# Last cross attention: where the value products, the totals and the context copies stand in a turn

## The chip, the cores and the metric

The kernel runs on one core of one Trainium2 chip. The metric is the device time of one execution in microseconds (us), lower is better. Engines: TensorE (PE, with its weight loads as PEld), VectorE (DVE), ScalarE (ACT), GpSimd (POOL), and SyncE (SP), which issues DMAs. Each engine works through its own list of instructions in order and waits on semaphores for the others.

## The reference, cut to what matters

The whole computation is four layers of cross attention and feed-forward on `x` of 8 x 256 x 128, all in float32. The change lies in the fourth layer's cross attention. Its context is `ctx_2048`, 8 x 1601 x 256, and a learned null key and value are added, so there are 1602 keys.

```python
HEADS, DH = (16, 64)
q = _split_heads(jnp.einsum('bnd,df->bnf', x, Wq))
kv = jnp.einsum('bmc,cf->bmf', context, Wkv)
k, v = jnp.split(kv, 2, axis=-1)
k, v = (_split_heads(k), _split_heads(v))
...
k = jnp.concatenate((nk, k), axis=-2)
v = jnp.concatenate((nv, v), axis=-2)
q = q * scale
sim = jnp.einsum('bhid,bhjd->bhij', q, k)
attn = jax.nn.softmax(sim, axis=-1)
out = jnp.einsum('bhij,bhjd->bhid', attn, v)
...
out = jnp.einsum('bnf,fd->bnd', out, Wout)
```

A layer norm of the result follows, and it is added to `x`.

## The kernel before

The stages of the kernel run one after the other; `cross3` (L2215) is the sixth of seven, and all of the change is in its class `KeyMajorAttention` (L1761). It works in 64 turns: one for each of 8 batches and 8 pairs of heads (`PAIRS`). In a turn the scores of a pair are made with the keys on the 128 partitions: 13 blocks of 128 keys, two heads of 64 rows each, 256 queries as columns. Two blocks are a chunk (`CHUNKS` = 7).

The work on one pair is spread over three turns. In turn i:
- `pe_score` makes the scores of pair i, chunk by chunk (26 matmuls, L1930, each on 64 of the array's rows) into two halves of `psS`. ScalarE copies each chunk to `prob` (`act_keep`, L2035), and VectorE takes the running maximum over chunks (`dve_raise`, L2101), then the last one over the two halves (`dve_peak`, L2107). A half of `psS` is used again when both have read it: score chunk s waits for the copy and the raise of chunk s - 2.
- For pair i - 1 the softmax is made. `pe_turn_peak` (L1944) transposes the maxima into `psO` (called `peaks`), `dve_shift` (L2113) reduces them over the keys, `pe_spread_shift` (L1951) spreads the negative maxima over the partitions, again in `psO`. VectorE adds them to the scores (`dve_lower`, L2122, four parts for each head), ScalarE takes the exponential (`act_exp`, L2041, eight parts), and GpSimd adds the exponentials up over the blocks (`pool_sums`, L2187 to L2198).
- For pair i - 2 the values are met: `pe_meet` (26 matmuls, L1975, each on 64 of the array's columns) into `psT[:, 1, 0:S]`, and `pe_total` (L1960, two matmuls with ones, on 64 columns) sums the exponentials over the partitions into `psO`. `dve_invert` (L2128) takes the reciprocal, and `dve_divide` (L2136) multiplies. So the totals need `psO`, which the shift of the next pair holds until VectorE has lowered all eight parts, and the transposes of the maxima wait for the reciprocal.
- `pe_project` makes what the next turns need, in two banks (`psT[:, 0]` and `psM`) in turn: keys (L1897) and queries (L1900) of pair i + 1, values (L1907) of pair i - 1, in turns 4 to 6 of a batch the transposes of the next batch's context (L1889), and in turn 2 the output projection of the batch before (L1913). `due(i, at)` says what is made at which of eight places of a turn; its place in the list and its number settle the bank, and the bank who copies it out: bank 1 is ScalarE's (`act_take`, L2013 to L2024), bank 0 is VectorE's (`dve_take`, L2079 and L2081), but values always go to ScalarE.

A turn has four rounds (`for g in range(4)` in `pe_run`). Round g issues: values of `MEETS[g]` (chunks 0 and 1, 2 and 3, 4 and 5, 6), in the first round the transposes of the maxima, then the projections due at place 2g, in the first round the spreading of the shift, then two chunks of scores, then the projections due at 2g + 1. The totals stand at the head of the third round. ScalarE in a round: the copies due at 2g, the copies of two score chunks, the copies due at 2g + 1; and in the first and second round four exponentials each. VectorE's order is written out in `dve_run`.

The accumulating value products of a pair all lie in one bank region, so the values of the next pair wait for the divide (`out_done`).

Of the kernel before, what the change touches and what calls it, by code (L numbers as in the profile page):

```python
# [1760 lines left out]
class KeyMajorAttention:  # L1761
# [16 lines left out]
    MEETS = [range(0, 2), range(2, 4), range(4, 6), range(6, 7)]  # L1778
# [46 lines left out]
    def due(self, i, at):  # L1825
# [7 lines left out]
        if 0 <= b < B - 1 and p in (4, 5, 6) and at in (2, 3, 4) and (p - 4) * 3 + at - 2 < 8:  # L1833
            names.append(("ctx", b + 1, (p - 4) * 3 + at - 2))
        if at == 3 and p == 2 and b > 0:
            names = (names or [None]) + [("out", b - 1, 0)]
# [97 lines left out]
    def pe_turn_peak(self, pe, i):  # L1934
        nc = self.k.nc
        pe.wait_ge(*self.peaked(i + 1))
        if i >= 2:
            pe.wait_ge(*self.inverted(i - 1))
# [15 lines left out]
    def pe_total(self, pe, i):  # L1954
        nc = self.k.nc
        pe.wait_ge(*self.summed(14 * (i + 1)))
        if i + 1 < self.TURNS:
            pe.wait_ge(*self.lowered(8 * (i + 2)))
        for h in range(2):
            last = nc.tensor.matmul(self.peaks[h * self.HD:(h + 1) * self.HD, 0:S], self.ones[:], self.acc[i % 2][:, h, 0:S],  # L1960
                                    start=True, stop=True)
# [17 lines left out]
    def pe_run(self, pe):  # L1979
# [4 lines left out]
        for i in range(-1, T + 3):  # L1984
            scores, softmax, meets = 0 <= i < T, 0 <= i - 1 < T, 0 <= i - 2 < T
            for g in range(4):
                if meets and g == 2:
                    self.pe_total(pe, i - 2)
                if meets:
                    for s in self.MEETS[g]:  # L1990
                        self.pe_meet(pe, i - 2, s)
                if softmax and g == 0:
                    self.pe_turn_peak(pe, i - 1)
                for name in self.due(i, 2 * g):
                    self.pe_project(pe, name)
                if softmax and g == 0:
                    self.pe_spread_shift(pe, i - 1)
                if scores:
# [8 lines left out]
    def act_take(self, act, name):  # L2007
# [13 lines left out]
        if kind == "ctx":  # L2021
            c, g = n // 4, n % 4
            w = BANK if g < 3 else KTAIL
            last = nc.scalar.copy(self.ctxT[of % 2][:, c, g * BANK:g * BANK + w], bank[:, 0:w])  # L2024
        last.then_inc(self.taken[self.number[name][0]].sem, 1)
# [22 lines left out]
    def act_run(self, act):  # L2048
# [3 lines left out]
        for i in range(-1, T + 1):  # L2052
            scores, softmax = 0 <= i < T, 0 <= i - 1 < T
            for g in range(4):
# [5 lines left out]
                if softmax and g < 2:  # L2060
                    for part in range(4):
                        self.act_exp(act, i - 1, g, part)
# [61 lines left out]
    def dve_invert(self, dve, i):  # L2124
# [3 lines left out]
        self.k.nc.vector.reciprocal(self.rtotal[:], self.peaks[:, 0:S]).then_inc(self.inverted.sem, 1)  # L2128
# [9 lines left out]
    def dve_run(self, dve):  # L2138
# [4 lines left out]
        for i in range(0, T + 3):  # L2143
# [12 lines left out]
            self.dve_take_at(dve, i, 2)  # L2156
            if softmax:
                self.dve_lower(dve, i - 1, 1, 2)
                self.dve_lower(dve, i - 1, 1, 3)
            if scores:  # L2160
# [1434 lines left out]
```

## Time and profile before

| | us |
|---|---|
| median of 3 runs | 4140.33 |
| lowest and highest | 4135.44, 4140.78 |
| profiled execution, device time | 4139.14 |
| its span in the trace | 4137.1 |
| TensorE busy in the span | 3676.2 (89%) |
| VectorE, ScalarE, GpSimd busy | 2683.1, 2281.6, 1350.8 |
| last cross attention, first scores to last divide | 2081.7 to 3874.2 |

Line numbers (L1975) are those of the kernel before. PE stands for matmuls, PEld for weight loads. Matmuls are pipelined, so their records overlap, and a float32 matmul leaves two records and two weight loads (the 26 value matmuls of a turn are 52 records). Where TensorE is busy all the time, the distances between the starts of neighbouring groups tell how long each group holds the engine.

### The profile page before, as it was taken

The numbers are of one execution on the slowest core, as the hardware profiler recorded it, in microseconds if no ns is written. First come the engines' busy times: TensorE is split into PE (matmuls) and PEld (weight loads), VectorE is DVE, ScalarE is ACT, GpSimd is POOL, SyncE is SP. The second block draws the span as 40 slices with busy tenths as digits, with TensorE's granted clock in tenths as the row PEclk, the third lists the DMA queues.
The fourth block names the chain that finished last, engine by engine and source line by source line (L and its number), as shares of the span: only waits on it lengthen the run. The fifth ranks groups of instructions, "written<-read, shape, count | busy, mean of one in ns | idle before, by whom it ended". The sixth has DMA issues, their size and how long they took to land. (4 is left out here: it accounts for less than half of the span.)

```text
span 4137.1 us, 72514 instructions
## 1 busy us (share of the span) xinstructions
PE 3676.2 (89%) x28012; PEld 2206.1 (53%) x28017; DVE 2683.1 (65%) x4526; ACT 2281.6 (55%) x3856; POOL 1350.8 (33%) x1655
## 2 busy tenths in 40 slices
PE   3699999889699985997799999999999999999654
PEld 2233333478444434674456666666666666666441
DVE  4799999544577736554356666666656666666647
ACT  2599999633377752222156566666656566656330
POOL 3011111220011104220045565555555556556310
PEclk7699999999799987998899999999999999999877
DMA  4332231002165401000100000000000000000010
GB/s 140 128 62 50 50 63 42 20 18 46 48 94 82 58 2 31 2 2 10 49 16 17 1 17 1 1 17 1 17 1 17 1 17 1 1 1 1 7 37 20
DMA packets 117718, 122.91 MB, mean 30 GB/s; under 512 B 19008, under 2 KB 95648, under 8 KB 116992
## 3 DMA queue, kind: packets, MB, share of 16 engines
q1 hardware_dynamic: 104184, 111.20, 12.2%
q10 hardware_dynamic: 13200, 7.16, 0.6%
q8 instruction: 221, 3.62, 0.4%
q14 instruction: 113, 0.93, 0.1%
HBM read 102.51 MB, written 15.68 MB: 29 GB/s over the span
## 5 line engine op out<-in xcount | busy, mean ns | idle before, releaser
L2101 DVE TENSOR_TENSOR att_highest.1<-att_highest.1,psS 128x1024 f32<-128x1024 f32 (+1 forms) x320 | 356.6, 1114 | 369.2 <-ACT prob_0.1 L2035 181.8
L869 DVE TENSOR_REDUCE att_peak.1<-psS 128x1 f32<-128x512 f32 (+1 forms) x1024 | 579.2, 633 | 19.8 <-PE psS L744 13.4
L839 ACT ACTIVATE att_probT.1<-psT 128x512 f32<-128x512 f32 (+1 forms) x682 | 366.6, 568 | 29.2 <-PE psT L773 9.9
L2192 POOL TENSOR_TENSOR key_sums_0.1<-key_sums_0.1,prob_0.1 128x512 f32<-128x512 f32 x256 | 326.5, 1275 | 28.7 <-POOL key_sums_0.1 L2192 0.4
L2192 POOL TENSOR_TENSOR key_sums_1.1<-key_sums_1.1,prob_1.1 128x512 f32<-128x512 f32 x256 | 325.8, 1273 | 28.7 <-POOL key_sums_1.1 L2187 0.4
L869 DVE TENSOR_REDUCE att_peak.2<-psS 128x1 f32<-128x512 f32 (+1 forms) x512 | 261.6, 568 | 78.7 <-PE psS L744 75.8
L790 PE MATMUL psM<-att_probT.1,quad_values.1 128*9 128x256 f32 (+1 forms) x3840 | 291.9, 382 | 0.2 <-issue 0.2
L744 PE MATMUL psS<-key_stack.1,query_stack.1 64*128 64x512 bf16 (+1 forms) x1024 | 253.6, 379 | 25.2 <-PEq L379 16.2
L2122 DVE TENSOR_TENSOR prob_0.1<-prob_0.1,psO 128x1024 f32<-128x1024 f32 (+1 forms) x256 | 244.0, 1016 | 49.0 <-PE psO L1951 49.0
L2122 DVE TENSOR_TENSOR prob_1.1<-prob_1.1,psO 128x1024 f32<-128x1024 f32 (+1 forms) x256 | 243.9, 1016 | 49.0 <-PE psO L1951 49.0
L2187 POOL TENSOR_TENSOR key_sums_0.1<-prob_0.1 128x512 f32<-128x512 f32 x64 | 82.0, 1282 | 576.1 <-ACT prob_0.1 L2041 576.1
L2035 ACT COPY prob_0.1<-psS 128x1024 f32<-128x1024 f32 (+1 forms) x224 | 203.8, 954 | 72.6 <-PE psS L1930 72.1
L2035 ACT COPY prob_1.1<-psS 128x1024 f32<-128x1024 f32 (+1 forms) x224 | 203.7, 954 | 71.8 <-PE psS L1930 71.4
L773 PE MATMUL psT<-query_stack.1,key_stack.1 64*128 64x256 bf16 x1279 | 212.9, 275 | 9.6 <-ACT att_probT.1 L839 9.5
L1897 PE MATMUL psM<-ctxT_0.1,wkv.1 128*128 128x512 f32 (+1 forms) x512 | 215.5, 544 | 2.7 <-ACT keyT_0.1 L2018 1.4
L1930 PE MATMUL psS<-qT_1.1,keyT_1.1 64*128 64x256 f32 x1664 | 214.5, 392 | 2.0 <-DVE att_highest.1 L2101 2.0
L1930 PE MATMUL psS<-qT_0.1,keyT_0.1 64*128 64x256 f32 x1664 | 214.5, 392 | 1.0 <-ACT keyT_0.1 L2018 0.7
L1907 PE MATMUL psT<-wkv.1,ctxT_1.1 128*128 128x128 f32 (+1 forms) x1664 | 214.7, 280 | 0.1
L1907 PE MATMUL psT<-wkv.1,ctxT_0.1 128*128 128x128 f32 (+1 forms) x1664 | 214.4, 280 | 0.0
L1907 PEld LDWEIGHTS psT<-wkv.1,ctxT_1.1 128*128 128x128 f32 (+1 forms) x1664 | 192.1, 187 | 37.5 <-issue 36.9
L1907 PEld LDWEIGHTS psT<-wkv.1,ctxT_0.1 128*128 128x128 f32 (+1 forms) x1664 | 192.1, 187 | 37.2 <-issue 36.1
L1897 PE MATMUL psM<-ctxT_1.1,wkv.1 128*128 128x512 f32 (+1 forms) x512 | 211.5, 536 | 0.0
(688 smaller groups left out, 7511.4 us busy)
## 6 DMA issues: line engine op xcount, KB each, us to landing
key_stack.1<-key_parts SPq DMA_DIRECT2D x384, 58.0 KB
key_stack.2<-key_parts SPq DMA_DIRECT2D x96, 200.1 KB
ctx_rows.1<-in_ctx_dram SPq DMA_DIRECT2D x8, 1536.0 KB
key_parts<-split_parts.2 SPq DMA_DIRECT2D x8, 1200.8 KB, 7.5
ctx_keys_0.1<-in_ctx_dram ACTq DMA_DIRECT2D x4, 768.0 KB
ctx_keys_1.1<-in_ctx_dram ACTq DMA_DIRECT2D x4, 768.0 KB
query_stack.1<-query_parts SPq DMA_DIRECT2D x192, 16.0 KB
ctx_values_0.1<-in_ctx_dram SPq DMA_DIRECT2D x4, 768.0 KB
```

The source lines that it names most:

```text
L744: self.k.nc.tensor.matmul(self.score_bank[m % 3][:, 0:w], self.queries(rows, g, h, s * P, P), self.keys(rows, g, h, c0, w), start=True, st ...
L773: last = self.k.nc.tensor.matmul(self.key_bank[(m + h) % 3][0:w, n * S:(n + 1) * S], self.keys(rows, g, h, col, w), self.queries(rows, g, ...
L790: last = self.k.nc.tensor.matmul(self.partial[32 * j:32 * j + self.hd + 1, :], self.vquad[0:w, q % 2, blk, j, :], self.probT[0:w, g % self ...
L839: self.k.nc.scalar.activation(probs[:, blks[0]:blks[-1] + 1, :].rearrange("p b q -> p (b q)"), bank[0:w, 0:len(blks) * S], ACT.Exp).then_i ...
L869: self.k.nc.vector.tensor_reduce(self.peak[:, 2 * h + s, c:c + 1], self.score_bank[m % 3][:, 0:w], AX_X, ALU.max).then_inc(self.peak_done. ...
L1897: last = nc.tensor.matmul(bank[:, 0:w], self.wkv[:, t, p * P:(p + 1) * P], self.ctxT[b % 2][:, t, n * BANK:n * BANK + w], start=(t == 0), ...
L1907: last = nc.tensor.matmul(bank[0:w, kb % 4 * P:(kb % 4 + 1) * P], self.ctxT[b % 2][:, t, kb * P:kb * P + w], self.wkv[:, t, at:at + P], st ...
L1930: last = nc.tensor.matmul(k.psS[:, 2 * (g % 2) + h, blk % 2 * S:(blk % 2 + 1) * S], self.keyT[i % 2][own, blk * P:(blk + 1) * P], self.qT[ ...
L2035: nc.scalar.copy(self.prob[i % 2][:, :, at:at + w], k.psS[:, 2 * (g % 2):2 * (g % 2) + 2, 0:w]).then_inc(self.kept.sem, 1)
L2101: self.k.nc.vector.tensor_tensor(own, old, new, ALU.max).then_inc(self.raised.sem, 1)
L2122: self.k.nc.vector.tensor_tensor(own, own, by, ALU.add).then_inc(self.lowered.sem, 1)
L2192: nc.gpsimd.tensor_tensor(acc, acc, own[:, h, c * BANK:(c + 1) * BANK], ALU.add).then_inc(self.summed.sem, 1)
```

## The change

- The values of a turn, all seven chunks of pair i - 2, are issued in one run at the turn's head, ahead of the transposes of the maxima. `MEETS` goes.
- The totals of pair i - 2 move from the head of the third round to the second round, behind its value projection and ahead of its scores. They are written to the second half of the values' bank, `psT[:, 1, S:2S]`, rather than to `psO`. Their wait for the lowering of the next pair goes, and so does the wait of the transposes of the maxima for the reciprocal.
- ScalarE makes two exponentials in each of the four rounds, not four in each of the first two.
- VectorE takes raises 2 and 3 ahead of the last two lowerings, then the reciprocal and the divide together, ahead of raises 4 and 5.
- The context transposes are due at places 0, 2 and 4 rather than 2, 3 and 4, the output projection at place 2 rather than 3. All of them come out in bank 1, and ScalarE copies them; VectorE takes none in the turns.

```diff
--- before.py
+++ after.py
@@ -1775,7 +1775,6 @@
     CHUNKS = (KB + 1) // 2
     NULL = KTAIL + 1
     KEYS = KB * P
-    MEETS = [range(0, 2), range(2, 4), range(4, 6), range(6, 7)]
 
     def __init__(self, k, mem):
         self.k = k
@@ -1830,9 +1829,9 @@
             names.append(("value", i - 1, at // 2))
         if at % 2 == 1 and i + 1 < self.TURNS:
             names.append(("key", i + 1, (3, 0, 1, 2)[at // 2]))
-        if 0 <= b < B - 1 and p in (4, 5, 6) and at in (2, 3, 4) and (p - 4) * 3 + at - 2 < 8:
-            names.append(("ctx", b + 1, (p - 4) * 3 + at - 2))
-        if at == 3 and p == 2 and b > 0:
+        if 0 <= b < B - 1 and p in (4, 5, 6) and at in (0, 2, 4) and (p - 4) * 3 + at // 2 < 8:
+            names.append(("ctx", b + 1, (p - 4) * 3 + at // 2))
+        if at == 2 and p == 2 and b > 0:
             names = (names or [None]) + [("out", b - 1, 0)]
         return names
 
@@ -1934,8 +1933,6 @@
     def pe_turn_peak(self, pe, i):
         nc = self.k.nc
         pe.wait_ge(*self.peaked(i + 1))
-        if i >= 2:
-            pe.wait_ge(*self.inverted(i - 1))
         if i >= 1:
             pe.wait_ge(*self.lowered(8 * i))
         for h in range(2):
@@ -1952,12 +1949,10 @@
         last.then_inc(self.spread.sem, 1)
 
     def pe_total(self, pe, i):
-        nc = self.k.nc
+        k, nc = self.k, self.k.nc
         pe.wait_ge(*self.summed(14 * (i + 1)))
-        if i + 1 < self.TURNS:
-            pe.wait_ge(*self.lowered(8 * (i + 2)))
         for h in range(2):
-            last = nc.tensor.matmul(self.peaks[h * self.HD:(h + 1) * self.HD, 0:S], self.ones[:], self.acc[i % 2][:, h, 0:S],
+            last = nc.tensor.matmul(k.psT[h * self.HD:(h + 1) * self.HD, 1, S:2 * S], self.ones[:], self.acc[i % 2][:, h, 0:S],
                                     start=True, stop=True)
         last.then_inc(self.totalled.sem, 1)
 
@@ -1983,18 +1978,19 @@
             self.pe_project(pe, ("ctx", 0, n))
         for i in range(-1, T + 3):
             scores, softmax, meets = 0 <= i < T, 0 <= i - 1 < T, 0 <= i - 2 < T
+            if meets:
+                for s in range(self.CHUNKS):
+                    self.pe_meet(pe, i - 2, s)
+            if softmax:
+                self.pe_turn_peak(pe, i - 1)
             for g in range(4):
-                if meets and g == 2:
-                    self.pe_total(pe, i - 2)
-                if meets:
-                    for s in self.MEETS[g]:
-                        self.pe_meet(pe, i - 2, s)
-                if softmax and g == 0:
-                    self.pe_turn_peak(pe, i - 1)
                 for name in self.due(i, 2 * g):
-                    self.pe_project(pe, name)
+                    if name is not None:
+                        self.pe_project(pe, name)
                 if softmax and g == 0:
                     self.pe_spread_shift(pe, i - 1)
+                if meets and g == 1:
+                    self.pe_total(pe, i - 2)
                 if scores:
                     for s in self.of_run(g):
                         self.pe_score(pe, i, s)
@@ -2022,6 +2018,8 @@
             c, g = n // 4, n % 4
             w = BANK if g < 3 else KTAIL
             last = nc.scalar.copy(self.ctxT[of % 2][:, c, g * BANK:g * BANK + w], bank[:, 0:w])
+        if kind == "out":
+            last = nc.scalar.copy(k.XN[:, of * QT:(of + 1) * QT, :].rearrange("p t d -> p (t d)"), bank[:, 0:S])
         last.then_inc(self.taken[self.number[name][0]].sem, 1)
 
     def act_keep(self, act, i, s):
@@ -2049,7 +2047,7 @@
         T = self.TURNS
         for n in range(1, 8, 2):
             self.act_take(act, ("ctx", 0, n))
-        for i in range(-1, T + 1):
+        for i in range(-1, T + 3):
             scores, softmax = 0 <= i < T, 0 <= i - 1 < T
             for g in range(4):
                 self.act_take_at(act, i, 2 * g)
@@ -2057,9 +2055,9 @@
                     for s in self.of_run(g):
                         self.act_keep(act, i, s)
                 self.act_take_at(act, i, 2 * g + 1)
-                if softmax and g < 2:
-                    for part in range(4):
-                        self.act_exp(act, i - 1, g, part)
+                if softmax:
+                    for part in (2 * g, 2 * g + 1):
+                        self.act_exp(act, i - 1, part // 4, part % 4)
 
 
 
@@ -2125,7 +2123,7 @@
         dve.wait_ge(*self.totalled(i + 1))
         if i >= 1:
             dve.wait_ge(*self.out_done(i))
-        self.k.nc.vector.reciprocal(self.rtotal[:], self.peaks[:, 0:S]).then_inc(self.inverted.sem, 1)
+        self.k.nc.vector.reciprocal(self.rtotal[:], self.k.psT[:, 1, S:2 * S]).then_inc(self.inverted.sem, 1)
 
     def dve_divide(self, dve, i):
         b, p = divmod(i, self.PAIRS)
@@ -2154,22 +2152,22 @@
                 self.dve_lower(dve, i - 1, 1, 0)
                 self.dve_lower(dve, i - 1, 1, 1)
             self.dve_take_at(dve, i, 2)
+            if scores:
+                self.dve_raise(dve, i, 2)
+            self.dve_take_at(dve, i, 3)
+            if scores:
+                self.dve_raise(dve, i, 3)
             if softmax:
                 self.dve_lower(dve, i - 1, 1, 2)
                 self.dve_lower(dve, i - 1, 1, 3)
-            if scores:
-                self.dve_raise(dve, i, 2)
-                self.dve_raise(dve, i, 3)
-            self.dve_take_at(dve, i, 3)
-            self.dve_take_at(dve, i, 4)
             if meets:
                 self.dve_invert(dve, i - 2)
+                self.dve_divide(dve, i - 2)
+            self.dve_take_at(dve, i, 4)
             if scores:
                 self.dve_raise(dve, i, 4)
                 self.dve_raise(dve, i, 5)
             self.dve_take_at(dve, i, 6)
-            if meets:
-                self.dve_divide(dve, i - 2)
             if scores:
                 self.dve_raise(dve, i, 6)
                 self.dve_peak(dve, i)
```

## Rows read from the trace of the kernel before

**Rows 1.** Busy time by stretches: stretch, length, busy us (records) by engine, PEclk, DMA share, GB/s.

```profile
2900.00:3100.00 200.00, 200.00 (x1375) 132.77 (x1374) 126.04 (x131) 121.15 (x173) 109.30 (x98) 1.00 0.03 9
```

**Rows 2.** Timeline of TensorE, an ordinary turn: start, busy us, engine, line, operation, out<-in, records.

```profile
3796.41 1.95 PE L1975 MATMUL psT<-prob_0.1,values_0.1 128*64 128x256 f32 x16
3798.29 0.66 PE L1944 MATMUL psO<-tables.1,att_peak.3 128*128 128x128 f32 x4
3798.78 1.95 PE L1907 MATMUL psT<-wkv.1,ctxT_1.1 128*128 128x128 f32 x16
...
3801.10 2.00 PE L1930 MATMUL psS<-qT_0.1,keyT_0.1 64*128 64x256 f32 x16
...
3804.10 1.95 PE L1975 MATMUL psT<-prob_0.1,values_0.1 128*64 128x256 f32 x16
3805.98 2.05 PE L1907 MATMUL psT<-wkv.1,ctxT_1.1 128*128 128x128 f32 x16
3807.96 2.00 PE L1930 MATMUL psS<-qT_0.1,keyT_0.1 64*128 64x256 f32 x16
3809.89 1.98 PE L1897 MATMUL psM<-ctxT_1.1,wkv.1 128*128 128x512 f32 x4
3811.80 0.65 PE L1960 MATMUL psO<-key_sums_0.1,att_ones.1 128*64 128x256 f32 x4
...
3814.11 2.05 PE L1907 MATMUL psT<-wkv.1,ctxT_1.1 128*128 128x128 f32 x16
...
3819.93 0.65 PE L1975 MATMUL psT<-prob_0.1,values_0.1 66*64 66x256 f32 x4
3820.52 0.65 PE L1907 MATMUL psT<-wkv.1,ctxT_1.1 128*65 128x128 f32 x4
3821.10 0.70 PE L1930 MATMUL psS<-qT_0.1,keyT_0.1 64*128 64x256 f32 x4
...
3823.65 1.95 PE L1975 MATMUL psT<-prob_1.1,values_1.1 128*64 128x256 f32 x16
```

**Rows 3.** Timeline of TensorE in turn 1, which has no values to meet.

```profile
2098.67 2.00 PE L1930 MATMUL psS<-qT_1.1,keyT_1.1 64*128 64x256 f32 x16
...
2101.58 1.95 PE L1907 MATMUL psT<-wkv.1,ctxT_0.1 128*128 128x128 f32 x16
2103.46 2.00 PE L1930 MATMUL psS<-qT_1.1,keyT_1.1 64*128 64x256 f32 x16
...
2115.57 0.70 PE L1930 MATMUL psS<-qT_1.1,keyT_1.1 64*128 64x256 f32 x4 [1.13 <-DVE att_highest.1 L2101]
```

**Rows 4.** Timeline of all engines in the last turns.

```profile
3828.33 2.00 PE L1930 MATMUL psS<-qT_1.1,keyT_1.1 64*128 64x256 f32 x16
...
3830.26 1.95 PE L1975 MATMUL psT<-prob_1.1,values_1.1 128*64 128x256 f32 x16
...
3866.45 3.67 PE L1975 MATMUL psT<-prob_1.1,values_1.1 128*64 128x256 f32 x32
...
3873.76 0.42 DVE L2136 TENSOR_TENSOR att_outT.3<-psT,att_rtotal.4 128x256 f32<-128x256 f32 x1 [0.47 <-PE psT L1975]
```

**Rows 5.** Timeline of VectorE and ScalarE in the ordinary turn of the second group.

```profile
3801.21 3.81 DVE L2122 TENSOR_TENSOR prob_1.1<-prob_1.1,psO 128x1024 f32<-128x1024 f32 x4 [1.53 <-PE psO L1951]
3802.28 1.93 ACT L2035 COPY prob_0.1<-psS 128x1024 f32<-128x1024 f32 x2 [0.93 <-PE psS L1930]
...
3804.94 1.22 DVE L2101 TENSOR_TENSOR att_highest.1<-prob_0.1,psS 128x1024 f32<-128x1024 f32 x1
...
3806.07 3.81 DVE L2122 TENSOR_TENSOR prob_1.1<-prob_1.1,psO 128x1024 f32<-128x1024 f32 x4
...
3810.19 2.55 DVE L2101 TENSOR_TENSOR att_highest.1<-att_highest.1,psS 128x1024 f32<-128x1024 f32 x2 [0.31 <-ACT prob_0.1 L2035]
...
3812.65 1.75 DVE L2128 RECIPROCAL att_rtotal.4<-psO 128x256 f32<-128x256 f32 x1
...
3820.78 0.42 DVE L2136 TENSOR_TENSOR att_outT.3<-psT,att_rtotal.4 128x256 f32<-128x256 f32 x1
```

## The prediction

> **What bounds the kernel now.** I read three views in this order. The busy time by stretches shows that in the last cross attention (2100 to 3820 us) TensorE is busy without a gap, at the full granted clock, while VectorE and ScalarE are busy about 0.63 and 0.61 of the time and GpSimd less [rows 1]. So what is taken off the other engines is worth nothing there, and only what shortens TensorE's own row of instructions counts. Busy time does not say whether TensorE is efficient, though: its records overlap. So I read, as the second view, the timeline of TensorE alone for one ordinary turn and took the distances from start to start [rows 2]. A turn runs from the first values at 3796.41 to the next turn's at 3823.65: 27.24 us. The third view is turn 1, whose rounds have no values in them, because nothing is there to meet yet [rows 3]: it is the nearest thing to a round of the changed kernel.
>
> **What a change of shape costs.** The values and the totals (L1975, L1960) use 64 columns of the array at a time, the scores (L1930) 64 rows, everything else the whole array. The distances of [rows 2] depend on the neighbour. Keys or values in the whole array behind one another cost nothing extra; behind or ahead of a 64-wide group they cost 0.05 to 0.10 us more. Piece by piece, old against new, for one turn:
> - Values and totals. Now 1.88 (3796.41 to 3798.29), 1.88 (3804.10 to 3805.98), 2.31 for the totals with the third group (3811.80 to 3814.11) and 0.59 (3819.93 to 3820.52): 6.66 us [rows 2]. In one run the 52 records cost less: 32 records are busy 3.67 us against 1.95 for 16 [rows 2, 4], so 16 more take 1.72 us, and 52 take 1.88 + 36 x 1.72 / 16 = 5.75 us. The totals alone have the four records of the last group, 0.59 us. New: 6.34. Saved 0.32.
> - The second and third value projections (L1907) no longer stand behind values: 1.98 (3805.98 to 3807.96) becomes the 1.88 of turn 1 (2101.58 to 2103.46) [rows 2, 3]. Twice 0.10, and half of it, 0.05, as an estimate for the short fourth one: 0.25.
> - Three key or query projections no longer stand ahead of a 64-wide group. From the first scores to the end of the query projection it is 3.00 now (3801.10 to 3804.10) and 2.91 in turn 1 (2098.67 to 2101.58) [rows 2, 3]. I give the key projection of 1.91 (3809.89 to 3811.80) and its like in the third round the same 0.09: 0.27.
> - The scores of the second round now follow the totals: from columns straight to rows. No row shows that step. From the whole array to the scores the cost is inside the 1.93 of each pair of score chunks, and from scores straight to values, the same step the other way round, the scores take 3828.33 to 3830.26, again 1.93 [rows 4], no less and no more than ahead of a key. I take the scores as unchanged; if the step were free the turn would be 0.20 shorter, and if it cost twice, 0.20 longer. Those are the two ends, and I stay in the middle because the nearest rows say that each step into or out of a 64-wide shape is paid once.
>
> The Trainium skill, TensorEngine Tiling (Array Packing), section Tiling Modes, says that changing the tiling mode drains the engine. The rows agree in sign, at 0.1 to 0.2 us for each visit, and by that rule the free step from totals to scores is the less likely end.
>
> Sum: 0.32 + 0.25 + 0.27 = 0.84 us a turn, from 27.24 to 26.40. It applies from the head of turn 2 to the head of turn 63: 61 turns, 51 us. The turns with context transposes or the output projection are longer by those alone, and keep them.
>
> **Is TensorE still never kept waiting?** This is where such a gain can vanish, because the rounds lose the values that gave the other engines time. I walked through the new turn from its head at 0. Values 5.75, peak transposes 0.49, value projection and shift 2.32 [rows 2]: first scores at 8.56. Then value projection 1 at 11.47, totals 13.35, scores 2 and 3 at 13.94, value projection 2 at 17.69, scores 4 and 5 at 19.57, the short value projection at 23.32, score 6 at 23.85, end at 26.40.
> - VectorE, from [rows 5]: it begins to lower 0.11 us behind the scores' start, at 8.67; the first raise follows 3.73 later, at 12.40, and must be over before score 3 at 14.9: it is at 13.6. Two lowerings to 15.8. Raise 2 needs ScalarE's copy, which starts 1.18 behind the scores (3802.28 against 3801.10) and takes half of 1.93: 16.1. Two raises, 2.55: 18.7. Two lowerings, a whole and a short one, about 1.5: 20.1. Reciprocal 1.75: 21.9. Divide 0.42: 22.3. Raise 4, about 1.2: 23.5, and score 6 needs it at 23.85. The slack is 0.2 to 0.3 us with the hand-over: enough, but the narrowest place of the whole change.
> - The reciprocal is now ahead of raise 4 and waits for the totals, and behind it stand the divide and raises 4 to 6. The totals are done at 13.9 and the reciprocal is due at 20.1: cover of 6 us. The totals need GpSimd's sums of the turn before last, and GpSimd is busy 0.55 of the time [rows 1]; its last sum is over some 7 us into the next turn by my walk, against 13.35.
> - ScalarE: two exponentials in each round rather than four in the first two. The copies of scores 2 and 3 no longer stand behind four of them. The copy of score 6 stands behind two and is late (about 26.8), raise 6 and the peak come to 28.3, and the transposes want that peak at 26.4 + 5.75 = 32.2: covered. The last exponentials (28.7 and 29.1) are wanted by values at 29.9 and 31.6: covered, and they would hold TensorE in the middle of the run if ScalarE were 1.2 us later.
> - The context and output copies that go from VectorE to ScalarE are 0.4 to 0.7 us each, three in a batch and one in a batch, on an engine busy 0.61. The two context transposes that move to another round have the same whole-array neighbours: nothing. Dropped waits (on the reciprocal, on the lowering of the next turn) free no time, since TensorE never stood in them in an ordinary turn; they only make the order possible. No DMA is moved.
>
> **The ends.** Turn 1 loses its stalls. From 2098.67 to 2115.57 it takes 16.90 us; the pieces without waits are 2.91 + 1.88 + 1.93 + 1.82 + 1.88 + 1.93 + 1.82 + 0.53 = 14.70 (1.82 is 1.91 less 0.09, 0.53 is 0.58 less 0.05), so 2.2 us are waits [rows 3]; with the new orders of VectorE and ScalarE I expect them gone. At the other end something is given back. After turn 62 there are no key projections, and the walk gives VectorE's chain 24.0 us for turn 63 where the old turn took 23.1. In turn 64 all thirteen value blocks stand ahead of the shift, so the last lowering, which starts the last exponentials and GpSimd's last sums, is 5.75 - 1.88 = 3.9 us later. The last divide (3873.76) [rows 4] no longer waits for values behind the totals: 0.5 back. Together 4.3 lost, 2.2 won: 2 lost, give or take 3.
>
> **The sum.** 51 - 2 = 49 us. The profiled execution took 4139.1 (a span of 4137.1 and 2.0 around it), 1.2 below the median of 4140.3, well within the 5.3 us between the three runs. From the median: 4091 us.
>
> **The rivals.**
> - Waits take the gain, and more: the slower side. Turn 1 shows that rounds without values can stall: 2.2 us, the last one a wait of 1.13 us for VectorE ahead of score 6 [rows 3]. If the new orders did not help and each turn kept these 2.2 us, a turn would be 1.36 us longer: 61 x 1.36 - 2 x 1.1, some +81, 4221 us. The place is score 6 behind raise 4; it turns to a loss once VectorE reaches raise 4 more than 0.2 + 0.84 = 1.0 us later than in my walk. For it: the reciprocal and the divide, 2.2 us, move ahead of raise 4. Against it: in turn 1 two more lowerings (1.5 us) stood ahead of raise 2, and four exponentials ahead of the copies of scores 2 and 3. Chance 0.05.
> - A small wait at score 6 (or in the values for the last exponential), 0.2 to 0.6 us a turn: 12 to 36 us of the 49 are lost, 4103 to 4127. The slack of 0.2 is no more than my rounding. Chance 0.12.
> - The change does not do what it says: the group costs reappear elsewhere and a turn stays near 27.24: 4140. The distances are the same to 0.01 us wherever the neighbours are, which speaks against it. Chance 0.03.
> - The joined run is no shorter, because each weight load of the same rows waits for the matmul before it: then the 0.40 of the joined values is missing, 61 x 0.40 = 24, 4115. Against it, 32 records are busy 3.67 us [rows 4], 0.11 each. Chance 0.02.
> - The step from totals to scores is free or other waits go: 4070 to 4080. Chance 0.05.
>
> By the Trainium skill, TensorE: Matmul & The Clock Gate, Part 3, The mechanism, a weight load overlaps matmuls in flight only when its row group differs; the values use all rows, so that rule would give the fourth rival. The record spacing above disagrees.
>
> **How the numbers follow.** The forecast, 4080 to 4103, has 0.73. With the rival of a small wait taken in to 4114 and 4078 below, the range holds somewhat over 8 in 10. Faster by over 0.2% (8 us, about what a measurement of this kernel can tell from no change): 0.73 + 0.12 + 0.02 + 0.05 = 0.92. Within 0.2%: 0.03. Slower: 0.05.
>
> **What the changed profile would show.** Ordinary turns of 26.40 us from values to values; one run of 52 value records of 5.75; totals to scores 0.6; TensorE still busy 1.00 in every stretch with no idle ahead of L1930. A turn of 26.6 with the scores of the second round at 2.1 would be a dearer step between the shapes. Idle time ahead of L1930 released by L2101 would be the waits; ahead of L1975 released by L2041, late exponentials. The prediction is wrong if the engines' chains, not TensorE's row, set the turn.

## The result, and the profile after

The changed kernel takes 4095.84 us (median of 4 runs, 4093.10 to 4105.07) against 4140.56 us before: a ratio of 0.9894, with a 95% interval from 0.9882 to 0.9906. It is faster by 1.1%. The forecast was 4091 in a range of 4078 to 4114. The profiled execution took 4095.66 us with a span of 4093.9, which is 43.2 below the span of 4137.1.

I read the same views as before, in the same order. First the busy time by stretches of the kernel after (stretch, length, busy us by engine, granted clock, DMA): TensorE is still busy all the time at the full clock, as in [rows 1], and VectorE and GpSimd are a little busier, mostly because the same work is packed into less time (GpSimd's operations are also a little longer; the last section says why). The last three lines are from the end of the stage and come up again below.

```profile
2900.00:3100.00 200.00, 200.00 (x1422) 139.26 (x1420) 129.40 (x130) 123.24 (x184) 119.24 (x105) 1.00 0.00 1
...
3795.00:3799.00 4.00, 4.00 (x24) 2.30 (x24) 2.35 (x3) 1.85 (x3) 3.70 (x4) 0.62 0.01 2
...
3815.00:3819.00 4.00, 3.81 (x24) 2.33 (x26) 0.14 (x1) 0.43 (x2) 3.75 (x4) 0.68 0.00 0
...
3828.00:3835.00 7.00, 6.35 (x32) 6.16 (x32) 0.00 (x0) 0.37 (x1) 0.00 (x0) 0.61 0.00 0
```

Then the timeline of an ordinary turn after, which answers [rows 2, 5] (start, busy us, engine, line, operation). L1970 are the values, L1955 the totals, L1929 the scores, L2099 the raises.

```profile
3744.85 5.83 PE L1970 MATMUL psT<-prob_0.1,values_0.1 128*64 128x256 f32 x52
...
3750.62 0.66 PE L1941 MATMUL psO<-tables.1,att_peak.3 128*128 128x128 f32 x4
...
3753.43 2.00 PE L1929 MATMUL psS<-qT_0.1,keyT_0.1 64*128 64x256 f32 x16
...
3756.34 1.95 PE L1906 MATMUL psT<-wkv.1,ctxT_1.1 128*128 128x128 f32 x16
...
3758.22 0.65 PE L1955 MATMUL psT<-key_sums_0.1,att_ones.1 128*64 128x256 f32 x4
...
3758.80 2.00 PE L1929 MATMUL psS<-qT_0.1,keyT_0.1 64*128 64x256 f32 x16
...
3760.73 1.98 PE L1896 MATMUL psM<-ctxT_1.1,wkv.1 128*128 128x512 f32 x4
...
3767.08 2.54 DVE L2099 TENSOR_TENSOR att_highest.1<-att_highest.1,psS 128x1024 f32<-128x1024 f32 x2
...
3768.71 0.70 PE L1929 MATMUL psS<-qT_0.1,keyT_0.1 64*128 64x256 f32 x4
...
3771.25 5.83 PE L1970 MATMUL psT<-prob_1.1,values_1.1 128*64 128x256 f32 x52
```

From values to values it is now 26.40 us. The run of values takes 5.77 (3744.85 to 3750.62), the totals 0.58, and the scores behind them 1.93, as behind any other group. Raise 4 starts 22.23 us into the turn, and no group of TensorE shows idle time ahead of it. The turns with context transposes or an output projection are longer than an ordinary one by the same amounts as before (1.31, 0.93, 0.49 and 3.57 us), so the new places of these gain and cost nothing on TensorE.

Where the 43.2 us of the span went, from the starts of the same records in both timelines:

| stretch | before | after | difference |
|---|---|---|---|
| up to the transposes of turn 1 | 2095.86 | 2096.60 | +0.7 |
| turn 1, to the first values | 22.26 | 20.05 | -2.2 |
| first values to the head of turn 63 (61 turns) | 1705.53 | 1654.60 | -50.9 |
| turn 63 | 23.07 | 23.85 | +0.8 |
| turn 64 to the last divide | 27.05 | 32.18 | +5.1 |
| last divide to the copy of the last output | 4.42 | 7.10 | +2.7 |
| the rest | 258.9 | 259.5 | +0.6 |

### The profile page after: what moved, and what is told of

The parts are those of the page before. It is cut to its first block and busy times, and to the rows that moved or that the text cites. A ratio compares the mean times of both kernels' runs of the same rounds, so it can differ in the third digit from the quotient of the medians.

```text
span 4093.9 us, 72451 instructions
## 1 busy us (share of the span) xinstructions
PE 3628.1 (89%) x28012; PEld 2230.9 (54%) x28017; DVE 2690.9 (66%) x4497; ACT 2263.1 (55%) x3885; POOL 1372.5 (34%) x1655
## 5 line engine op out<-in xcount | busy, mean ns | idle before, releaser
L2099 DVE TENSOR_TENSOR att_highest.1<-att_highest.1,psS 128x1024 f32<-128x1024 f32 (+1 forms) x320 | 356.1, 1113 | 191.2 <-ACT prob_0.1 L2033 102.6
L2190 POOL TENSOR_TENSOR key_sums_1.1<-key_sums_1.1,prob_1.1 128x512 f32<-128x512 f32 x256 | 335.9, 1312 | 122.3 <-ACT prob_1.1 L2039 98.1
L2190 POOL TENSOR_TENSOR key_sums_0.1<-key_sums_0.1,prob_0.1 128x512 f32<-128x512 f32 x256 | 336.3, 1314 | 95.8 <-ACT prob_0.1 L2039 71.7
L2111 DVE TENSOR_REDUCE att_shift.4<-psO 128x4 f32<-128x512 f32 x64 | 44.3, 692 | 283.9 <-PE psO L1941 283.9
L1906 PEld LDWEIGHTS psT<-wkv.1,ctxT_1.1 128*128 128x128 f32 (+1 forms) x1664 | 199.3, 187 | 35.8 <-issue 31.4
L1906 PEld LDWEIGHTS psT<-wkv.1,ctxT_0.1 128*128 128x128 f32 (+1 forms) x1664 | 199.8, 187 | 34.0 <-issue 32.4
L1896 PE MATMUL psM<-ctxT_0.1,wkv.1 128*128 128x512 f32 (+1 forms) x512 | 215.6, 544 | 2.7 <-ACT keyT_0.1 L2014 1.4
L1929 PE MATMUL psS<-qT_1.1,keyT_1.1 64*128 64x256 f32 x1664 | 214.5, 392 | 3.3 <-DVE att_highest.1 L2099 3.2
L2039 ACT ACTIVATE prob_1.1<-prob_1.1 128x1024 f32<-128x1024 f32 (+1 forms) x256 | 216.2, 898 | 1.2 <-DVE prob_1.1 L2120 1.1
L2039 ACT ACTIVATE prob_0.1<-prob_0.1 128x1024 f32<-128x1024 f32 (+1 forms) x256 | 216.1, 898 | 0.0
L1929 PE MATMUL psS<-qT_0.1,keyT_0.1 64*128 64x256 f32 x1664 | 214.5, 392 | 1.0 <-ACT keyT_0.1 L2014 0.7
```

Source lines behind the costliest of these rows:

```text
L1896: last = nc.tensor.matmul(bank[:, 0:w], self.wkv[:, t, p * P:(p + 1) * P], self.ctxT[b % 2][:, t, n * BANK:n * BANK + w], start=(t == 0), ...
L1906: last = nc.tensor.matmul(bank[0:w, kb % 4 * P:(kb % 4 + 1) * P], self.ctxT[b % 2][:, t, kb * P:kb * P + w], self.wkv[:, t, at:at + P], st ...
L1929: last = nc.tensor.matmul(k.psS[:, 2 * (g % 2) + h, blk % 2 * S:(blk % 2 + 1) * S], self.keyT[i % 2][own, blk * P:(blk + 1) * P], self.qT[ ...
L2039: self.k.nc.scalar.activation(own, own, ACT.Exp).then_inc(self.exped.sem, 1)
L2099: self.k.nc.vector.tensor_tensor(own, old, new, ALU.max).then_inc(self.raised.sem, 1)
L2190: nc.gpsimd.tensor_tensor(acc, acc, own[:, h, c * BANK:(c + 1) * BANK], ALU.add).then_inc(self.summed.sem, 1)
```

## The experiments

Each is the changed kernel with the edit shown, and all were compared with the kernel before on their own chip. There its median was 4139.3 us for the split values, both old orders and the earlier shift, and 4142.5 for the last three, so between rows the ratios and the stretches count more than a difference of 2 or 3 us of the medians. The table collects them; "61 turns" is the distance from the first values to the head of turn 63. Turn and stretch come from the timelines.

| kernel | median us | ratio to before | turn | 61 turns | head of turn 63 to last divide |
|---|---|---|---|---|---|
| before | 4140.6 | | 27.24 | 1705.5 | 50.1 |
| after | 4095.8 | 0.989 | 26.40 | 1654.6 | 56.0 |
| values split | 4140.0 | 1.000 (0.999 to 1.001) | 27.24 | 1705.9 | 51.3 |
| old exponentials | 4147.5 | 1.002 (1.001 to 1.003) | 27.15 | 1703.1 | 56.9 |
| old VectorE order | 4093.4 | 0.990 (0.988 to 0.992) | 26.40 | 1654.5 | 56.5 |
| divide twice | 4100.8 | 0.991 (0.989 to 0.993) | 26.59 | 1663.8 | 56.5 |
| totals in round three | 4107.6 | 0.992 (0.990 to 0.993) | 26.59 | 1666.4 | 56.0 |
| earlier shift in turn 64 | 4090.3 | 0.988 (0.986 to 0.989) | 26.40 | 1654.6 | 52.0 |
| totals at the head | 4080.8 | 0.985 (0.984 to 0.986) | 26.25 | 1645.2 | 52.1 |

**The values in four groups again.**

```diff
-            if meets:
-                for s in range(self.CHUNKS):
-                    self.pe_meet(pe, i - 2, s)
             for g in range(4):
+                if meets:
+                    for s in self.MEETS[g]:
+                        self.pe_meet(pe, i - 2, s)
+                    if g == 3:
+                        self.pe_total(pe, i - 2)
...
-                if meets and g == 1:
-                    self.pe_total(pe, i - 2)
```

Reciprocal and divide go behind raise 5 with it.

> The changed kernel with one part undone: the values stand in four groups again, one in each round, with the totals directly behind the last group (round four), and the reciprocal and the divide behind raise 5. The new exponential order and the absence of the old waits stay. Theory (the gain is TensorE's own cost of changing between 64-wide and whole-array groups): three more groups cost 0.99 us a turn by the record distances (0.144 for each key projection ahead, 0.20 and 0.20 and 0.15 for values and the value projection behind), the totals now ride with values and give 0.15 back, so an ordinary turn takes 27.24 us, as before the change, and the kernel 4096 + 61 x 0.84 = about 4147 less up to 5 at the end. Rival (the gain came from waits that went, or from the new orders on the other engines): the turn stays near 26.4 us and the kernel near 4096.

The timeline of TensorE in that kernel, from values to values:

```profile
3791.17 1.95 PE L1971 MATMUL psT<-prob_0.1,values_0.1 128*64 128x256 f32 x16
...
3800.74 2.05 PE L1907 MATMUL psT<-wkv.1,ctxT_1.1 128*128 128x128 f32 x16
3802.72 2.00 PE L1930 MATMUL psS<-qT_0.1,keyT_0.1 64*128 64x256 f32 x16
...
3814.26 0.65 PE L1971 MATMUL psT<-prob_0.1,values_0.1 66*64 66x256 f32 x4
3814.75 0.60 PE L1956 MATMUL psT<-key_sums_0.1,att_ones.1 128*64 128x256 f32 x4
3815.28 0.65 PE L1907 MATMUL psT<-wkv.1,ctxT_1.1 128*65 128x128 f32 x4
...
3818.41 0.87 PE L1971 MATMUL psT<-prob_1.1,values_1.1 128*64 128x256 f32 x6
```

The turn is 27.24 us again, with the new places of the exponentials and without the old waits, and the second value projection is back at 1.98. The whole gain in the turns goes with the grouping; the waits that went and the new orders give none of it by themselves. The kernel took 4140.0, somewhat below what was expected, in part because with short groups the end takes 51.3 rather than 56.0.

**ScalarE's exponentials in the old order.**

```diff
-                if softmax:
-                    for part in (2 * g, 2 * g + 1):
-                        self.act_exp(act, i - 1, part // 4, part % 4)
+                if softmax and g < 2:
+                    for part in range(4):
+                        self.act_exp(act, i - 1, g, part)
```

> The changed kernel with ScalarE's exponentials in the old order: four in the first and four in the second round. Theory (TensorE is not kept waiting only because the other engines' orders were changed with it): by the walk ScalarE's copy of scores 2 comes 0.8 us later, raise 4 comes 0.8 to 1.3 us later against a slack of 0.26 us, so each turn stalls ahead of L1929 by 0.6 to 1.1 us; turn 27.0 to 27.5, kernel 4096 + 61 x 0.85 = about 4148 (4133 to 4163). Rival (the order on an engine that is busy 0.6 of the time is worth nothing): 4096.

The waits of TensorE in that kernel from 2100 to 3760 us (who waited for whom, us in total, times, longest), and one of its turns, which begins with the values at 3766.27:

```profile
PE psS L1929 <- DVE att_highest.1 L2099: 31.9, 47, 1.6
PE psM L1896 <- ACT ctxT_1.1 L2020: 6.8, 8, 0.8
PE psM L1896 <- ACT ctxT_0.1 L2020: 5.1, 6, 0.9
```

```profile
3778.34 3.25 ACT L2039 ACTIVATE prob_0.1<-prob_0.1 128x1024 f32<-128x1024 f32 x4
...
3781.95 1.94 ACT L2033 COPY prob_1.1<-psS 128x1024 f32<-128x1024 f32 x2
...
3784.64 3.45 ACT L2039 ACTIVATE prob_0.1<-prob_0.1 128x1024 f32<-128x1024 f32 x4
...
3788.46 1.93 ACT L2033 COPY prob_1.1<-psS 128x1024 f32<-128x1024 f32 x2
...
3789.51 2.55 DVE L2099 TENSOR_TENSOR att_highest.1<-att_highest.1,psS 128x1024 f32<-128x1024 f32 x2 [0.36 <-ACT prob_1.1 L2033]
...
3790.88 0.70 PE L1929 MATMUL psS<-qT_1.1,keyT_1.1 64*128 64x256 f32 x4 [0.69 <-DVE att_highest.1 L2099]
```

The first four exponentials stand ahead of the copy of scores 2, which starts 1.74 us behind the second scores' start (3780.21) rather than 1.18. The second four stand ahead of the copy of scores 4, which starts 2.62 us behind its scores (3785.84), again rather than 1.18. VectorE's chain is late by the first, 0.56 us, and then waits 0.36 for the second copy: raise 4 starts 23.24 us into the turn, 1.01 later than after the change, and score 6 waits. The turn is 27.15, and 61 turns cost 48.5 us, nearly all of the 50.9 that the grouping had gained (expected: 52). Turn 1 is long again too: 22.81 us up to the first values, where the changed kernel takes 20.05. Changing the order on an engine that is busy 0.6 of the time gains nothing in the ordinary turns by itself and yet keeps nearly the whole gain.

**VectorE's order as before.** The lowerings ahead of raises 2 and 3, the reciprocal ahead of raise 4, the divide behind raise 5:

```diff
+            if softmax:
+                self.dve_lower(dve, i - 1, 1, 2)
+                self.dve_lower(dve, i - 1, 1, 3)
             if scores:
                 self.dve_raise(dve, i, 2)
...
                 self.dve_invert(dve, i - 2)
-                self.dve_divide(dve, i - 2)
...
                 self.dve_raise(dve, i, 5)
...
+            if meets:
+                self.dve_divide(dve, i - 2)
```

> The changed kernel with VectorE's order as before: all lowerings ahead of raises 2 and 3, the reciprocal ahead of raise 4, the divide behind raise 5. Theory by the walk: raise 2 starts 1.2 us later (17.35 in the turn) and raise 3 ends at 19.9, wanted at 20.5; the reciprocal follows, raise 4 waits for its copy at 21.8 and ends at 23.0, wanted at 23.7. Nothing is late, turn 26.40, kernel 4096, no change. Rival (VectorE's new order was needed, as the exponentials' was): stalls ahead of score 4 or 5, turn above 26.6, kernel above 4108.

The turn is 26.40 and the kernel took 4093.4: no difference from 4095.8 that these runs can show (their intervals overlap). VectorE's timeline there shows why: raise 4 even starts earlier in the turn, at 21.80 (3761.39, with values at 3739.59), and waits for its copy.

```profile
3739.59 5.83 PE L1970 MATMUL psT<-prob_0.1,values_0.1 128*64 128x256 f32 x52
...
3761.39 2.54 DVE L2099 TENSOR_TENSOR att_highest.1<-att_highest.1,psS 128x1024 f32<-128x1024 f32 x2 [0.32 <-ACT prob_0.1 L2033]
```

So that part of the change is idle: this order has more slack at score 6 than the new one, and turn 1 is 20.15 with it, against 20.05.

**The slack at score 6.** The divide is done twice, the first time into a spare tile:

```diff
+        if again:
+            self.k.nc.vector.tensor_tensor(self.spare[:], self.k.psT[:, 1, 0:S], self.rtotal[:], ALU.mult).then_inc(self.spared.sem, 1)
+            dve.wait_ge(*self.spared(self.again + 1))
+            self.again += 1
```

> The changed kernel with the divide done twice on VectorE (the first time into a spare tile), ahead of raise 4; nothing else. It measures the slack of VectorE's chain, which the profile after gives as 0.26 us: raise 4 ends at 3768.30 and score 6, started at 3768.71, could start 0.15 behind it. Theory: an operation of 0.42 us with its own wait puts raise 4 back by 0.5 us, so an ordinary turn gets 0.25 us longer (26.65) with idle ahead of L1929 released by L2099; the 14 turns with a context transpose in their third round have 0.44 us more slack and stay. 47 x 0.25 = 12 us, kernel 4096 + 12 = 4108 (4103 to 4114). Rival (slack of 0.5 or more): 4096.

```profile
3749.92 5.83 PE L1972 MATMUL psT<-prob_0.1,values_0.1 128*64 128x256 f32 x52
...
3772.60 2.54 DVE L2101 TENSOR_TENSOR att_highest.1<-att_highest.1,psS 128x1024 f32<-128x1024 f32 x2
3773.96 0.70 PE L1931 MATMUL psS<-qT_0.1,keyT_0.1 64*128 64x256 f32 x4
```

Raise 4 starts 22.68 into the turn, 0.45 later than after the change, and the turn is 26.59, 0.19 longer; so the slack was 0.26 us, as read from the profile. The turns with a context transpose in the third round (27.71 and 27.33) are unchanged. So short a wait is not listed as a wait on L2101, because the matmul records overlap across it; only the distance shows it. In all 9.2 us in 61 turns, and a kernel of 4100.8, 2 below the expected range and 7 below the 4108 forecast. The turns explain 3 of the 7: the added wait cost 0.19 a turn rather than 0.25. In the profiled execution 4 more lie ahead of the stage, which begins at 2092.6 rather than 2096.6, and that is within what executions differ by (2091.4 to 2096.6 in the nine profiled ones).

**The totals in the third round.**

```diff
+                if meets and g == 2:
+                    self.pe_total(pe, i - 2)
                 for name in self.due(i, 2 * g):
...
-                if meets and g == 1:
-                    self.pe_total(pe, i - 2)
```

> The changed kernel with the totals (into their new place) at the head of the third round, between two whole-array projections, as in the kernel before. Theory (each visit to a 64-wide shape pays once, and columns straight to rows pays as any other): the totals then cost 0.144 ahead of them and 0.20 behind, against 0.144 and 0.007 more than projection to scores now: 0.19 us a turn, 26.59, kernel 4096 + 12 = 4108. Rival (the step from columns to rows is dearer than average and the third round would be the better place): turn at or below 26.40, kernel 4096 or less.

```profile
3755.23 5.83 PE L1970 MATMUL psT<-prob_0.1,values_0.1 128*64 128x256 f32 x52
...
3772.44 0.65 PE L1955 MATMUL psT<-key_sums_0.1,att_ones.1 128*64 128x256 f32 x4
3773.02 2.05 PE L1906 MATMUL psT<-wkv.1,ctxT_1.1 128*128 128x128 f32 x16
3775.00 2.00 PE L1929 MATMUL psS<-qT_0.1,keyT_0.1 64*128 64x256 f32 x16
...
3781.83 0.44 PE L1970 MATMUL psT<-prob_1.1,values_1.1 128*64 128x256 f32 x2
```

26.60 from values to values, and 4107.6: both as expected. Between two whole-array projections the totals make a visit of their own, and the value projection behind them takes 1.98 again. Behind a projection and ahead of scores they share the step with the scores. One step more costs 0.19 us a turn, so the step from columns straight to rows is neither free nor dearer than the others.

**The shift earlier in turn 64.** In the one turn behind the last scores, three value chunks stand ahead of the transposes and four behind the shift:

```diff
+            ahead = 3 if i == T else self.CHUNKS
             if meets:
-                for s in range(self.CHUNKS):
+                for s in range(ahead):
                     self.pe_meet(pe, i - 2, s)
...
+                if meets and g == 0:
+                    for s in range(ahead, self.CHUNKS):
+                        self.pe_meet(pe, i - 2, s)
```

> The changed kernel, except in turn 64, the one behind the last scores: only three of the seven value chunks stand ahead of the transposes of the maxima, four behind the spreading of the shift. Theory (the 5.9 + 2.7 us given back at the end come from the last lowering starting later behind the whole run of values, and from TensorE's clock falling to half while it waits): the shift comes 2.3 to 3.1 us earlier, and the last divide with it; the kernel takes 3 us less, up to 6 if the clock falls less. About 4093 (4090 to 4094). Rival (the end is set by the halved clock alone): no change within 1 us.

In that kernel, first TensorE at the head of turn 64 (timeline), then the busy time by stretches:

```profile
3793.80 0.70 PE L1929 MATMUL psS<-qT_1.1,keyT_1.1 64*128 64x256 f32 x4 [3.00 <-DVE att_highest.1 L2103]
3794.44 2.81 PE L1970 MATMUL psT<-prob_0.1,values_0.1 128*64 128x256 f32 x24
```

```profile
3795.00:3799.00 4.00, 4.00 (x38) 3.03 (x35) 2.42 (x3) 1.39 (x3) 3.70 (x4) 1.00 0.01 2
...
3815.00:3819.00 4.00, 0.65 (x6) 0.15 (x2) 0.00 (x0) 0.00 (x0) 3.56 (x5) 1.00 0.00 0
...
3823.00:3828.00 5.00, 4.84 (x30) 4.87 (x31) 0.01 (x1) 0.00 (x0) 0.00 (x0) 0.69 0.00 0
```

The distance to the last divide falls from 56.0 to 52.0, and the granted clock stays at 1.00 where it had been 0.62 and 0.68: both runs of values are at full speed (5.9 and 5.8 us). The output projection stays slow: 5.2 us, at 0.69. The 4.0 is more than the 2.3 to 3.1 that the earlier shift alone was given, but 1.7 of it is the first run of values at full speed, and that the edit doesn't explain. It changes nothing ahead of those values, and TensorE stood idle for the same 3.00 us just before them, here as in the changed kernel. With one profiled execution of each, this part is luck as far as is known. What is left, 2.3, is what the earlier shift gave. In the profiled execution 2.1 us come back behind the last divide (268.7 against 266.6 from its start to the end), so its span is only 2.6 shorter; the medians are 5.5 apart, but their runs reach over each other (4083.7 to 4093.3, 4093.1 to 4105.1). That the end is shorter is shown; how much of it the kernel keeps is not.

**A version that goes further.** The totals of pair i - 3 stand at the head of turn i, straight ahead of the values, in the bank of the maxima; ScalarE copies the finished values out; reciprocal and divide move into VectorE's idle time at the head; and turn 64 is as in the experiment above.

```diff
+            if 0 <= i - 3 < T:
+                self.pe_total(pe, i - 3)
             if meets:
                 for s in range(ahead):
                     self.pe_meet(pe, i - 2, s)
...
+        act.wait_ge(*self.met(self.CHUNKS * (i + 1)))
+        if i >= 2:
+            act.wait_ge(*self.out_done(i - 1))
+        self.k.nc.scalar.copy(self.held[i % 2][:], self.k.psT[:, 1, 0:S]).then_inc(self.moved.sem, 1)
...
+            if 0 <= i - 3 < T:
+                self.dve_invert(dve, i - 3)
+                self.dve_divide(dve, i - 3)
             if softmax:
                 self.dve_shift(dve, i - 1)
```

> A version that goes further. The totals of pair i - 3 stand at the head of turn i, directly ahead of the run of values, in the bank of the maxima, which is free there; so they cost no visit of their own. For that ScalarE copies the finished values of a pair out of their bank (0.4 us, ahead of its first copy of a turn), and VectorE takes reciprocal and divide at the head of the next turn, where it is idle for 4.5 us, and no longer ahead of raise 4. The end of turn 64 is that of the earlier kernel with three value chunks ahead. Theory: 0.15 us a turn less by the record distances, 26.25, 61 x 0.15 = 9, and 3 to 6 at the end: about 4083 (4078 to 4087), and no idle ahead of any TensorE group. Rival (the peak transposes wait for the reciprocal, or the values for ScalarE's copy): turn at 26.4 or above, kernel 4090 or more.

```profile
3731.03 0.65 PE L1962 MATMUL psO<-key_sums_1.1,att_ones.1 128*64 128x256 f32 x4
...
3731.51 5.78 PE L1977 MATMUL psT<-prob_0.1,values_0.1 128*64 128x256 f32 x52
...
3734.72 1.13 DVE L2153 TENSOR_TENSOR att_outT.3<-att_held_1.1,att_rtotal.4 128x256 f32<-128x256 f32 x1
...
3757.28 0.65 PE L1962 MATMUL psO<-key_sums_0.1,att_ones.1 128*64 128x256 f32 x4
```

26.25 us from totals to totals, as worked out, and 4080.8 us: 0.985 of the kernel before (0.984 to 0.986). That is 15 us below the changed kernel by the medians; in the profiled executions 9.4 of it are in the 61 turns and 3.9 at the end. The totals at the head take 0.48, since the values follow in the same shape.

## Why the prediction was right

- **What bounds the stage**: TensorE's own row of instructions. Right; the split values undo all of the gain in the turns.
- **The cost of a change of shape**: 0.84 a turn forecast, 1705.53 - 1654.60 = 50.93 over 61 turns, 0.835 each, measured. The ordinary turn came out at 26.40, as forecast, and so did the terms of the sum: the run of values took 5.77 (5.75 forecast), the totals 0.58 (0.59), the second and third value projections 1.88 each, from scores to the end of the query projection 2.91. So this is no sum that came right by errors that cancel.
- **Totals to scores**, the one step without a row: taken as an ordinary one, and it is. Both ends of that range fell away. The rule of the Trainium skill, TensorEngine Tiling (Array Packing), Tiling Modes, that a change of tiling mode drains the engine, agrees here with the 1.93 of the scores behind the totals.
- **Slack at score 6**: 0.2 to 0.3 forecast; the profile after gives 0.26, and an added 0.45 made the turn 0.19 longer. The walk had raise 4 start at 22.3, and it started at 22.23.
- **The waits rival** (turn 1's stalls in each turn) did not come, but it was real: with the old exponentials the turn is 27.15 and the kernel 0.2% slower than before (0.1 to 0.3). The prediction gave the new orders of both engines the credit for keeping TensorE fed. The runs give it to ScalarE's alone; with VectorE's old order everything stays. The walk named score 6 behind raise 4 as the narrowest place, and it is; but it looked for the danger in VectorE's reciprocal and divide, for which the room was enough (0.26 us are left).
- **Turn 1** gave 2.2 us, as forecast, and it too goes with ScalarE's order: 22.81 with the old exponentials, 20.15 with VectorE's old order, 20.05 after the change.
- **The end** is where the forecast of 49 for 43.2 went wrong. The term was 4.3 us lost; the end lost 0.8 + 5.1 + 2.7 = 8.6. Turn 63 cost 0.8 (0.9 forecast). The rest of the term missed TensorE's clock. Its groups at the end, in the timeline of the kernel after, with the last line of the kernel before for comparison:

```profile
3795.10 7.52 PE L1970 MATMUL psT<-prob_0.1,values_0.1 128*64 128x256 f32 x52
3802.55 0.66 PE L1941 MATMUL psO<-tables.1,att_peak.3 128*128 128x128 f32 x4
...
3815.19 7.52 PE L1970 MATMUL psT<-prob_1.1,values_1.1 128*64 128x256 f32 x52 [2.37 <-DVE att_outT.3 L2134]
...
3827.85 6.49 PE L1912 MATMUL psM<-wout.1,att_outT.3 128*128 128x128 f32 x32 [2.41 <-DVE att_outT.3 L2134]
```

```profile
3874.33 3.81 PE L1913 MATMUL psT<-wout.1,att_outT.3 128*128 128x128 f32 x32 [0.69 <-DVE att_outT.3 L2136]
```

  TensorE stood idle for 3.0 us in turn 63, 2.4 us ahead of the last values, 2.1 ahead of the last totals and 2.4 ahead of the output projection. The granted clock was 0.62, 0.68 and 0.61 of full in the stretches that follow: for part of them to the lower of its two levels, 1.2 GHz. The values of turn 64 take 7.45 rather than 5.77, 1.7 us ahead of the shift; the last output projection takes 6.5 rather than 3.85, 2.7 us. Together 4.4, and that is the miss of this term. The slow values of turn 65 cost nothing, because the last totals waited for GpSimd behind them.

  The two parts are not equally sure. The slow output projection comes with the change: in all eight changed kernels TensorE stood idle for 2.4 us ahead of it, and it took 5.2 to 6.5 us. In the kernel before, the last totals stood ahead of the last 20 value records, so the reciprocal ran beside values, TensorE was idle for 0.69 us, and the projection took 3.81. The slow values of turn 64 came in six of the eight. They did not come in the last version, which was idle for 0.9 us there, nor with the earlier shift, which was idle for the same 3.00 us as the changed kernel. So an idle stretch is not followed by the lower clock each time, and what decides it stays open. The kernel before had such a fall as well, behind 3.9 us of idle time in turn 64 (16 value records in 3.4 us rather than 1.9, a granted clock of 0.67 from 3860 to 3865), but the totals that came next waited for GpSimd, and it cost nothing.
- The other 1.4 us of the miss lie outside the stage (+0.7 and +0.6). In the nine profiled executions the stage's first transposes start at 2091.4 to 2096.6, and from the copy of the last output to the end it takes 258.7 to 262.8, so this is no more than what executions differ by; what sets it stays open.

## What to carry to other kernels

Where a profile shows TensorE busy all the time, read the distances from start to start between groups, not the busy time. A visit to a 64-wide shape between whole-array work costs 0.3 us in all here; joining such groups, or putting one beside another 64-wide group, saves that or a part of it in each turn. Before doing so, walk the other engines through the denser round. The walk finds the narrowest place, but only undoing one order at a time shows which one matters: here it was ScalarE's, the engine that the walk worried about less. Look at the ends apart: what is joined delays what the tail waits for, and a tail in which TensorE stands idle for 2 or 3 us can lose half of its clock for a while, which cost 4.4 us here.

## What the runs showed of the hardware

VectorE operations that read two operands from SBUF are longer when they fall beside GpSimd's sums, and the rows show by how much. In 2200 to 3700 us the maximum over the two halves takes 0.69 before the change, where it falls between GpSimd's operations, and 0.99 after it, where it falls beside them, each time within 0.02 us (instruction, count, shortest, median and longest ns; kernel before, then after):

```profile
L2107 DVE TENSOR_TENSOR att_peak.3<-att_highest.1 x54: 691/691/693, 2200.7 to 3683.4; 128x512 f32<-128x512 f32 x54
```

```profile
L2105 DVE TENSOR_TENSOR att_peak.3<-att_highest.1 x55: 981/992/998, 2225.5 to 3693.0; 128x512 f32<-128x512 f32 x55
```

A raise of the same size, which reads one operand from SBUF and one from PSUM, takes 0.687 in the mean in both kernels, and after the change all 55 of them fall beside GpSimd's sums. One maximum of the kernel after, with the sums around it:

```profile
3745.01 1.28 POOL L2190 TENSOR_TENSOR key_sums_0.1<-key_sums_0.1,prob_0.1 128x512 f32<-128x512 f32 x1
3745.85 0.99 DVE L2105 TENSOR_TENSOR att_peak.3<-att_highest.1 128x512 f32<-128x512 f32 x1
...
3746.37 1.60 POOL L2190 TENSOR_TENSOR key_sums_0.1<-key_sums_0.1,prob_0.1 128x512 f32<-128x512 f32 x1
```

The sum that is running when the maximum starts has 0.44 us left, and the maximum is 0.30 longer than alone. The sum that starts while the maximum runs has 0.47 us of it ahead, and is 0.33 longer than the usual 1.27. In both directions the one that starts later is delayed by what is left of the other, less 0.14 us. The same holds for the maxima of all nine profiled executions wherever more than 0.15 us was left (0.32 to 0.65 us left with the values split, up to 1.00 with the old exponentials), each within 0.01 us. It holds in the last version for the divide from a copy in SBUF: 0.85 us left, 1.13 us long where it took 0.42 from PSUM. GpSimd's sums go from 1.273 to 1.314 us in the mean, because one of a pair's eight is the longer one. It cost nothing here: VectorE is idle for 4.5 us behind the maximum.

The Trainium skill, SBUF — State Buffer, section Who interferes with whom, says that a VectorE instruction with two inputs in SBUF contends with a GpSimd instruction that reads SBUF, and calls the port pair that the two share an exclusive lock. The trace agrees, with the delays above: each waits for the end of the other's whole operation, and not for a share of it.
